# 24 split tiles per chunk in a three-layer interaction kernel, 14 of their low parts on GpSimd

## What is computed

```python
e = jnp.stack([tbl_0[ids[:, 0]], ..., tbl_38[ids[:, 38]]], axis=1)      # (2048, 39, 16)
x0 = xk = e
for idx, (W, b) in enumerate([(w0, b0), (w1, b1), (w2, b2)]):
    z = relu(jnp.einsum('bhd,bkd,hks->bsd', x0, xk, W) + b[None, :, None])
    if idx != 2:
        xk = z[:, :64, :]
        direct.append(z[:, 64:, :])
    else:
        direct.append(z)
z = jnp.sum(jnp.concatenate(direct, axis=1), axis=-1)
h = jnp.concatenate([z, dense_ctx], axis=1)
h = jnp.maximum(h @ W_top1 + b_top1, 0.0)
h = jnp.maximum(h @ W_top2 + b_top2, 0.0)
y = h @ W_top3
```

## Time and profile before

| | before |
|---|---|
| median of 3 runs | 2626.81 us (2619.22 to 2628.51) |
| profiled execution | 2621.27 us, span 2619.4 us |
| TensorE matmul (PE) busy | 2487.5 us, 95% |
| VectorE (DVE) busy | 2452.1 us, 94% |
| ScalarE (ACT) busy | 866.4 us, 33% |
| GpSimd (POOL) busy | 973.6 us, 37% |
| DMA | 469.76 MB, 179 GB/s |
| granted TensorE clock, mean | 0.99 of full |

### The profile page before, as it was taken

How to read it: one execution, slowest core, us unless ns; L and a number is a source line. 1 busy time by engine, 2 the same in 40 slices (tenths; PEclk the granted TensorE clock), 3 DMA queues, 4 the chain that set the end, 5 groups by cost and what they waited for, 6 DMA issues and landing times.

```text
span 2619.4 us, 28223 instructions
## 1 busy us (share of the span) xinstructions
PE 2487.5 (95%) x7350; PEld 1370.7 (52%) x7350; DVE 2452.1 (94%) x2375; ACT 866.4 (33%) x853; POOL 973.6 (37%) x674
## 2 busy tenths in 40 slices
PE   0699999999999999999999999999999999999978
PEld 0355555555555555555555555555555555555546
DVE  2599999999999999999999999999999999999982
ACT  0133333233333323333332333333233333333325
POOL 7570542608163360726336071633607262000000
PEclk9899999999999999999999999999999999999999
DMA  3997888998888898888888988888898788888710
GB/s 82 224 213 176 193 176 194 193 201 193 182 189 179 191 194 196 197 181 192 179 192 188 205 195 181 187 178 190 188 204 214 163 188 177 191 181 195 176 46 8
DMA packets 184305, 469.76 MB, mean 179 GB/s; under 512 B 37746, under 2 KB 74211, under 8 KB 184275
## 3 DMA queue, kind: packets, MB, share of 16 engines
q1 hardware_dynamic: 160941, 461.79, 78.2%
q0 software_dynamic: 19968, 5.15, 2.1%
q10 hardware_dynamic: 3367, 2.48, 0.4%
HBM read 456.96 MB, written 12.33 MB: 179 GB/s over the span
## 4 chain that ended last, share of the span: by engine, by line
PE 38%; DVE 28%; DMA 15%; issue 13%; ACT 2%; SPq 1%; DVEq 1%; POOL 0%; ACTq 0%
PE zacc_a L811 17%; PE zacc_b L811 15%; DMA spread<-x_periods 14%; DVE prod L705 13%; DVE low L676 7%; DVE prod L693 5%; PE zacc_a L846 2%; PE zacc_b L846 2%; DVE high L676 1%; ACT maps L549 1%; DMA shifted<-x_periods 1%; ACT high L578 1%; ACT maps L548 1%; SPq L422 1%; DVE half L712 1%
## 5 line engine op out<-in xcount | busy, mean ns | idle before, releaser
L705 DVE TENSOR_TENSOR prod<-spread,maps 128x1024 f32<-128x1024 f32 (+1 forms) x1280 | 1493.8, 1208 | 27.8 <-DMA spread<-x_periods 18.0
L578 ACT ACTIVATE high<-prod 128x1024 fp32r<-128x1024 f32 (+2 forms) x544 | 575.0, 1057 | 1452.8 <-DVE prod L705 1207.0
L483 POOL DMA_INDIRECT landed<-in_tbl,rows_id x624 | 953.3, 1528 | 237.5 <-issue 235.5
L811 PE MATMUL zacc_a<-prod,w_plain 128*128 128x512 f32 (+2 forms) x1920 | 881.9, 595 | 19.7 <-DVE prod L693 15.0
L811 PE MATMUL zacc_b<-prod,w_plain 128*128 128x512 f32 (+2 forms) x1920 | 877.9, 593 | 5.3 <-DVE prod L705 5.3
L676 DVE TENSOR_TENSOR low<-prod,high 128x1024 fp32r<-128x1024 f32 (+1 forms) x480 | 581.7, 1212 | 0.0
L811 PEld LDWEIGHTS zacc_a<-prod,w_plain 128*128 128x128 f32 (+2 forms) x1920 | 363.8, 190 | 362.3 <-issue 328.1
L811 PEld LDWEIGHTS zacc_b<-prod,w_plain 128*128 128x128 f32 (+2 forms) x1920 | 363.9, 190 | 347.3 <-issue 308.4
L489 POOL TENSOR_TENSOR mark<-mark 128x1 f32<-128x1 f32 x30 | 16.6, 553 | 973.2 <-PE maps L858 967.6
L693 DVE TENSOR_TENSOR prod<-shifted,x_thrice 117x1024 f32<-117x1024 f32 (+1 forms) x224 | 264.8, 1214 | 50.8 <-DMA shifted<-x_periods 49.3
L846 PE MATMUL zacc_a<-low,w_high 128*128 128x512 f32 (+1 forms) x480 | 234.8, 570 | 12.2 <-DVE low L676 12.2
(11 more groups left out here) (101 smaller groups left out, 821.7 us busy)
## 6 DMA issues: line engine op xcount, KB each, us to landing
spread<-x_periods SPq DMA_DIRECT2D x608, 512.0 KB, 22.9
shifted<-x_periods SPq DMA_DIRECT2D x640, 156.0 KB
x_thrice<-x_periods SPq DMA_DIRECT2D x96, 156.0 KB
landed<-in_tbl,rows_id POOLq DMA_INDIRECT x624
x_periods<-x SPq DMA_DIRECT2D x32, 256.0 KB
spread<-x_periods SPq DMA_DIRECT2D x32, 256.0 KB, 26.3
features<-feat ACTq DMA_DIRECT2D x16, 128.0 KB, 5.4
spread<-features SPq DMA_DIRECT2D x4, 512.0 KB, 5.4
```

Of the source, the lines that this page charges most:

```text
L483: nc.gpsimd.indirect_dma_start(out=landed[:, f, :], out_offset=None, in_=tables[f], in_offset=bass.IndirectOffsetOnAxis(ap=rows_id[:, f:f ...
L578: nc.scalar.activation(high[0:rows, h, :], prod[0:rows, p, :], ACT.Copy).then_inc(s_round, 1)
L705: nc.vector.tensor_tensor(to, spread[0:rows, t, :], maps[0:rows, :], ALU.mult).then_inc(s_prod, 1)
L811: return nc.tensor.matmul(z[:, hf * BANK:(hf + 1) * BANK], w, x[:, hf * BANK:(hf + 1) * BANK], start=start, stop=stop)
```

## The change

The plan gets a third kind, **P**, a split tile whose low part is made on GpSimd instead of VectorE. Per chunk there are now 23 F, 10 V and 14 P (before 30 F and 17 V): 7 P and 3 V in layer 1 and in layer 2 each, 4 V in layer 0. The ring `high` gets 4 slots. GpSimd's 39 gathers are spread over 39 slots of the two chunks: every tile of layer 0 from tile 21 of the even chunk on, and 26 tiles of layers 1 and 2 that are not P. The new row numbers are taken at tile 20 (`GATHER_AT`) instead of 16. The sums of layer 2 move to tiles 21 to 23 (`SUM2_AT`), with waits for the sums placed before them, the feature addition to tile 24, and the store of the features to tile 30 (`KEEP_AT`). At the start the gathers of the second group are dealt out in the same way.

```diff
-PLAN = "FVFFVFFVFFVFFVFFFVFV" "FVFVFVF" "FVFFVFFVFFVFFVFFFVFV"
-NP, NH = 8, 3
+PLAN = "FPFVPFFPFPFVPFFPFPFV" "FVVFVVF" "FPFVPFFPFPFVPFFPFPFV"
+SPLIT = "VP"
+NP, NH = 8, 4
...
-KEEP_AT = 14
-TURN_AT, COPY_AT, WRITE_AT, GATHER_AT = 13, 15, 16, 16
+KEEP_AT = 30
+SUM01_AT, SUM2_AT = N1 + LZ + 2, N1 + 1
+TURN_AT, COPY_AT, WRITE_AT, GATHER_AT = 13, 15, 16, 20
...
+def gather_slots():
+
+    free = [p for p in range(GATHER_AT + 1, 2 * TILES) if PLAN[p % TILES] != "P"]
+    among = [p for p in free if p % TILES in SQUARED]
+    rest = [p for p in free if p % TILES not in SQUARED]
+    need = FIELDS - len(among)
+    return sorted(among + [rest[i * len(rest) // need] for i in range(need)])
...
+        def low_done(turn, j):
+
+            return (s_lowv if PLAN[j] == "V" else s_lowp), n_kind(turn, j, PLAN[j]) + 1
...
+            def low_part(turn, j):
+                rows, at_ = rows_of(j), slot(j, ALL, NP)
+                pool.wait_ge(s_round, n_kind(turn, j, SPLIT) + 1)
+                nc.gpsimd.tensor_tensor(low[0:rows, at_, :], prod[0:rows, at_, :], high[0:rows, slot(j, SPLIT, NH), :],
+                                        ALU.subtract).then_inc(s_lowp, 1)
...
+                    numbers(turn.shift(3), 1)
+                    gather(0, 12)
+                if PLAN[j] == "P" and has(turn, j):
+                    low_part(turn, j)
+                if turn.fixed and turn.number() == -1 and j in SQUARED:
+                    gather(12 + 2 * (j - N1), 14 + 2 * (j - N1))
+                if turn.fixed and turn.number() == 0 and j < 13:
+                    gather(26 + j, 27 + j)
+                fetched = turn.shift(3 if turn.odd else 4)
+                if fetched.real() and (not turn.fixed or turn.number() >= 0):
+                    if j == GATHER_AT and not turn.odd:
+                        numbers(fetched, fetched.group(1, 0))
+                    if turn.odd * TILES + j in GATHERS:
+                        f = GATHERS.index(turn.odd * TILES + j)
+                        gather(f, f + 1)
...
-                if PLAN[j] == "V" and has(turn, j):
-                    h, p, rows = slot(j, "V", NH), slot(j, ALL, NP), rows_of(j)
+                if PLAN[j] in SPLIT and has(turn, j):
+                    h, p, rows = slot(j, SPLIT, NH), slot(j, ALL, NP), rows_of(j)
...
-                        act.wait_ge(s_lowv, n_kind(*was, "V") + 1)
+                        act.wait_ge(*low_done(*was))
...
                     dve.wait_ge(ready, turn.count(1, 1))
+                    if which == 1:
+                        dve.wait_ge(s_sum01, turn.count(1, 1))
+                    elif not turn.fixed or turn.number() > 0:
+                        dve.wait_ge(s_sum2, turn.count(1, 0))
...
-                if last.real() and 0 <= j - LZ - 2 < 3:
-                    channel_sum(last, 1, j - LZ - 2)
-                if last.real() and last.odd and j == LZ + 5:
+                sum2_at = LZ + 2 if turn.fixed and turn.number() == CHUNKS else SUM2_AT
+                if last.real() and 0 <= j - sum2_at < 3:
+                    channel_sum(last, 1, j - sum2_at)
+                if last.real() and last.odd and j == sum2_at + 3:
                     feature(last, 1)
...
-                pe.wait_ge(s_lowv, n_kind(turn, j, "V") + 1)
+                pe.wait_ge(*low_done(turn, j))
```

More of the change, by code:

```diff
@@ L229, in build @@
         s_lowv = sem("s_lowv")
+        s_lowp = sem("s_lowp")
         s_mm = sem("s_mm")
@@ L273, in tail @@
         def tail(of):
-            split = [j for j in of if PLAN[j] == "V"]
+            split = [j for j in of if PLAN[j] in SPLIT]
             return split[-1] if split and split[-1] + LATE >= of[-1] else None
@@ L479, in _, with gather @@
             nc.gpsimd.memset(mark[:, :], 0.0).then_inc(s_mark, 1)
-            def gather():
-                for f in range(FIELDS):
+            def gather(first, last):
+                for f in range(first, last):
                     nc.gpsimd.indirect_dma_start(
@@ L489, in touch, with numbers @@
                 nc.gpsimd.tensor_tensor(mark[:, 0:1], mark[:, 0:1], mark[:, 1:2], ALU.add).then_inc(s_mark, 1)
-            def later(n, group):
+            def numbers(n, group):
                 pool.wait_ge(s_turned, n.group(1, 0))
@@ L505, in emit @@
                     pool.wait_ge(s_first, 16)
-                    gather()
+                    gather(0, FIELDS)
                     pool.wait_ge(s_all, 16)
[L508 to L511, removed]
+                    numbers(turn.shift(3), 1)
[13 more added lines that the diff above has]
+                        gather(f, f + 1)
             turns(pool, emit, GROUPS - 2)
@@ L573, in emit @@
                         act.wait_ge(s_prod, n_prod(turn, j) + 1)
-                    was = before(turn, j, "V", NH)
+                    was = before(turn, j, SPLIT, NH)
                     if was:
-                        act.wait_ge(s_lowv, n_kind(*was, "V") + 1)
+                        act.wait_ge(*low_done(*was))
                         act.wait_ge(s_mm, (n_late if stacked(was[1]) else n_tile)(*was) + 1)
@@ L647, in prepare @@
                     if stacked(j):
[L648 to L650 removed]
+                        nc.vector.memset(w_low[HALF:128, rank(j, SPLIT), :].bitcast(f32), 0.0)
+                        nc.vector.tensor_copy(w_high[HALF:128, rank(j, SPLIT), :], staged_tile(j))
+                    last = nc.vector.tensor_copy(w_high[0:rows_of(j), rank(j, SPLIT), :], staged_tile(j))
                 if split:
@@ L672, in low_part @@
                 rows = rows_of(j)
-                whole, top = prod[0:rows, slot(j, ALL, NP), :], high[0:rows, slot(j, "V", NH), :]
-                dve.wait_ge(s_round, n_kind(turn, j, "V") + 1)
-                to = high[HALF:128, slot(j, "V", NH), :] if stacked(j) else low[0:rows, slot(j, ALL, NP), :]
+                whole, top = prod[0:rows, slot(j, ALL, NP), :], high[0:rows, slot(j, SPLIT, NH), :]
+                dve.wait_ge(s_round, n_kind(turn, j, SPLIT) + 1)
+                to = high[HALF:128, slot(j, SPLIT, NH), :] if stacked(j) else low[0:rows, slot(j, ALL, NP), :]
                 nc.vector.tensor_tensor(to, whole, top, ALU.subtract).then_inc(s_lowv, 1)
@@ L740, in emit @@
                     low_part(then, i)
-                if turn.real() and 0 <= j - N1 - LZ - 2 < 3:
-                    channel_sum(turn, 0, j - N1 - LZ - 2)
-                if turn.real() and turn.odd and j == N1 + LZ + 5:
+                if turn.real() and 0 <= j - SUM01_AT < 3:
+                    channel_sum(turn, 0, j - SUM01_AT)
+                if turn.real() and turn.odd and j == SUM01_AT + 3:
                     feature(turn, 0)
@@ L870, in emit @@
                     then = step_back(turn, j, LATE)
-                    if then and PLAN[then[1]] == "V":
+                    if then and PLAN[then[1]] in SPLIT:
                         done = contract_low(*then)
```

21 lines of the change are left out of this document (11 added, 10 removed).

## The result

The changed kernel takes 2749.04 us (median of 4 runs, 2741.49 to 2757.46) where the kernel before, measured beside it, takes 2623.01: a ratio of 1.0483, with a 95% interval from 1.044 to 1.0526. It is slower by 126 us; the forecast was 2605, slightly faster, and the time lies above the range too, and above the range of rival B (up to 2730).

What follows compares the result with a forecast made beforehand. VectorE and TensorE were taken as tied, with TensorE the bound after the change: 145.2 us of work plus 5.4 of take waits make 150.6 us per turn against 152.0, 22 us over 16 turns, about 2605 us (2550 to 2705).

Steps and rivals of the forecast that it cites:

- rival B: GpSimd's low parts (tiles 17, 28) come late, shut out by VectorE: 6 us per turn, about 2685 us; chance 0.36.
- the low part on GpSimd: One 128x1024 low part made on GpSimd was put at 2.4 us, 28 of them per turn.
- The wait at tile 24: TensorE waits 1.82 us per chunk for the high part of tile 24, queued behind ScalarE's take of layer 1.
- TensorE's work of 145.2 us per turn: TensorE's work falls by 4.3 us to 145.2 us, as 14 tiles per turn go from plain to split.
- the term for the wait at tile 31: After the take of layer 0, TensorE waits 0.88 us per chunk for the high part of tile 31.
- The 4.94 us: Time from TensorE's next load after layer 0 completes, through ScalarE's take and next high part, to its consumer's load.
- the whole gain of 1.4: The turn of the loop was to fall from 152.0 to 150.6 us, 1.4 us less.
- the sum: Over the loop, 1.4 us per turn for 16 turns, 22 us less, giving about 2605 us.
- the moves put at nothing: Moved sums, their new waits and the late feature store cost nothing; the sums add 1.15 us to the squares' stretch.
- VectorE's lead of up to 6 tiles: In tiles 20 to 26, this lead pays for VectorE's 12.5 us of work against 10.7 for TensorE's tiles.
- nothing is added at start and end: Start and end gain only 7 small weight splits, which lie beside DMA waits.
- the loads dismissed by their busy share: DMA keeps about 14 MB per chunk; its busy share of 0.85 to 0.86 would stand at 0.87.

Runs made afterwards that it cites:

- short low parts: Changed kernel with GpSimd's low parts cut from 1024 to 32 columns, TensorE's late matmuls of those tiles reading the high part: 2650.1 us (ratio 1.0109).
- the run at 2520 us: Changed kernel with plain tiles behind the takes, GpSimd's low parts cut to 32 columns and spread loads halved: 2520.5 us (ratio 0.9591).
- the version with 17 splits: Changed kernel with 17 split tiles per chunk, 10 low parts on GpSimd: 2632.6 us; with sums back at tiles 6 to 8, store at 14: 2601.5 us.
- that version: Changed kernel with plain tiles behind the takes and GpSimd's low parts cut to 32 columns, spread loads whole: 2614.9 us (ratio 0.997).

## Why the prediction was wrong

*Held*: the low part on GpSimd, 2.4 us, was 2387 ns in the median. (The estimate from the ratio in the Trainium skill, "GPSIMD Engine Reference", section 3.1, was the same 2.4; the trace agrees.) The wait at tile 24, 1.82 us, was 1.94 in even chunks and 1.5 in odd ones (1.93 with short low parts). TensorE's work of 145.2 us per turn is right: the run at 2520 us has turns of 145.7 us.

*Failed, the term for the wait at tile 31.* The prediction put it at 0.88 us in each chunk. Its count starts the take when layer 0 is complete. The take stands behind the high part of tile 30, and that waits for VectorE's product of tile 30, a few tiles after VectorE itself was let go by the take of layer 1. The take starts 1.2 and 1.9 us late with short low parts and 2.8 and 3.4 in the changed kernel, and the waits at 30 and 31 are 2.1 and 3.0, and 3.8 and 4.5 us. The 4.94 us that the prediction counts from tile 28 to the consumer of the high part came from the kernel before, where tile 30 is plain and ScalarE had been idle for 1.30 us when the take started; the new plan has a split tile there. The mis-sizing without the port is 5.1-1.8 = 3.3 us per turn, more than the whole gain of 1.4.

*Right mechanism, too small and in the wrong place, rival B.* VectorE's two-operand instructions and GpSimd's reading ones exclude each other. I saw it shut GpSimd out, from the earlier trace rows, and counted late low parts on GpSimd. It also shuts VectorE out, for 116 us in all; neither the sum nor rival B has a term for that. In the changed kernel it can be watched both ways, in an odd chunk at the end of layer 1; GpSimd first:

```profile
1338.87 0.94 POOL L503 DMA_INDIRECT landed<-in_tbl,rows_id  x1 [0.30 <-issue]
1340.19 9.41 POOL L525 TENSOR_TENSOR low<-prod,high 128x1024 fp32r<-128x1024 f32 x2 [0.38 <-ACT high L614]
```

VectorE beside it:

```profile
1343.31 2.34 DVE L729 TENSOR_TENSOR prod<-shifted,x_thrice 117x1024 f32<-117x1024 f32 x2
1345.58 0.67 DVE L752 TENSOR_TENSOR half<-direct 128x512 f32<-128x512 f32 x1
1346.18 1.21 DVE L729 TENSOR_TENSOR prod<-shifted,x_thrice 117x1024 f32<-117x1024 f32 x1
1347.42 3.27 DVE L712 TENSOR_TENSOR high<-prod,high 64x1024 fp32r<-64x1024 f32 x1
```

Two low parts on GpSimd last 9.41 us instead of 4.8. The second stands still while squares and a sum follow each other without a gap; behind the gap of 0.03 us before 1347.42 it works, and now VectorE's low part of 1.2 us lasts 3.27. The Trainium skill ("SBUF — State Buffer", "Who interferes with whom") has the shared port as an exclusive lock; the trace agrees. It doesn't show that the earlier start wins: the second low part starts at 1342.53 in the trace, 0.78 us before the first square. This scene costs TensorE 2.3 us where it occurs, but on average only some 0.6 per turn, and the run with tile 17 on VectorE, which takes it away, changes nothing. The price is paid elsewhere: VectorE comes late to tile 27, so tile 30's product, the take and tile 31 are late. Of the 8.3 us there, 5.1 are there with short low parts and 3.2 need the long ones; without any gathers 8.0 remain, so they aren't a matter of the gathers in GpSimd's queue.

*Missing, the clock.* TensorE's pause of 3.2 us at tile 31 is often followed by a stretch at half the clock. Windows of the changed kernel: before the pause, the pause, after it, and later (PEclk is the third figure from the end):

```profile
1204.00:1210.60 6.60, 6.60 (x22) 3.89 (x21) 6.60 (x9) 3.39 (x4) 5.87 (x4) 1.00 0.98 201
1210.70:1213.70 3.00, 0.31 (x2) 0.00 (x0) 3.00 (x4) 2.95 (x3) 2.40 (x2) 1.00 1.06 202
1214.10:1217.50 3.40, 3.40 (x7) 1.95 (x6) 3.00 (x3) 1.91 (x2) 3.24 (x3) 0.50 1.01 212
1217.60:1225.00 7.40, 7.40 (x25) 4.51 (x24) 5.24 (x5) 2.12 (x2) 7.05 (x5) 1.00 1.05 221
```

From 150 us to some 110 us before the end there are 18 such stretches at 1.2 GHz (a granted clock of 0.50), 68 us together; in the kernel before, whose longest pause in the loop is 1.8 us, only one, of 6.8 us in the last chunk, which the changed kernel has too. Of the 25 pauses of 3.2 us at tile 31, 15 were followed or met by one. The eight loads from tile 31 on (tiles 31 and 32) took 3.97 us in the one shown, against 2.33 where the clock stayed at 2.4 GHz. That is a part of the table's last row.

*Wrong, the moves put at nothing*: the moved parts cost 19 us alone, and the place of sums and store 31 us in the version with 17 splits. The reason given, VectorE's lead of up to 6 tiles, was the ring's limit and not a lead that it has: VectorE was the bound, so it had little.

*Wrong, "nothing is added at start and end"*: what stands ahead of the loop and its first turn lose 23 us, 15 of which go when the gathers are left out.

*Wrong, the loads dismissed by their busy share.* At 0.85 of DMA time they looked harmless. What seems to count (argued, not shown) is that a stream of ten pieces, each let go by a product of layer 2, must end before the last products of layer 1; the faster the chunk, the less room. Shown is only that half of their bytes takes 94 us off that version. The forecast didn't fail by it, but an engineer who mended the takes alone would have.

*Open*: whether the gathers' 1.8 us per turn are a matter of GpSimd's queue or of the port; what the low clock costs by itself, as no run changes it alone; and whether a placing exists in which 24 splits pay with real low parts; half of the spread loads together with long low parts in such a placing wasn't tried.

## What to carry to other kernels

When two engines are tied at 98%, more work moved off one of them isn't a gain but a test of every chain between the others: write out for each in-order queue what stands before the instruction on which the bound engine waits next, and whom that waits for. Count an engine's lead from the trace, not from the size of its ring. Before giving GpSimd elementwise work, list VectorE's instructions with two SBUF operands in the same stretch: each meeting can cost one of the two up to a whole instruction of the other. Here a sum of 0.27 us lasted 2.44.

## What the runs showed of the hardware

A chained VectorE instruction with two operands in SBUF seems to reserve the port while the one ahead of it still runs: the gather of the earlier trace rows at 1070.02 was held although the low part beside it began only at 1070.97, and so was GpSimd's low part of 1342.53 by a square of 1343.31. Indirect DMA issue on GpSimd is held by plain two-operand fp32 instructions of VectorE: it lasts 0.94 us alone and up to 6.42 us beside them, in the kernel before, in which GpSimd makes no low parts. And after pauses of TensorE of 3.2 us its clock was often at 1.2 GHz for 3.4 us, and after pauses of 2.4 us at tile 26 in the run with plain tiles behind the takes too; after pauses of up to 1.8 us in the loop of the kernel before it stayed at 2.4 GHz.
